# Second attention layer: added key blocks, quarter masks, and another order of VectorE's and GpSimd's work

## What is computed

```python
x = _layernorm(x + L0_attn(x))     # 16 heads of 8, queries and keys RMS-normed
x = _layernorm(x + L0_ffn(x))      # top-1 routing over 16 experts of 320 slots
x = _layernorm(x + L1_attn(x))     # causal attention, d_k 8, d_v 64
x = _layernorm(x + L1_ffn(x))      # three coupling cycles

def L1_attn(x):                    # x: [16, 256, 128], 16 heads
    scores = einsum('bhqd,bhkd->bhqk', q, k) / sqrt(8)
    scores = where(causal, -inf, scores)
    ctx = einsum('bhqk,bhkd->bhqd', softmax(scores), v)
    return ctx.transpose(0, 2, 1, 3).reshape(B, T, 16 * 64) @ Wo
```

## Time and profile before

| | us |
|---|---|
| median of 3 runs | 951.15 (950.95 to 953.62) |
| the profiled execution | 950.26 |
| its span | 948.5 |

### The profile page before, as it was taken

How to read it: one execution, slowest core, us unless ns; L and a number is a source line. 1 busy time by engine, 2 the same in 40 slices (tenths; PEclk the granted TensorE clock), 3 DMA queues, 4 the chain that set the end, 5 groups by cost and what they waited for, 6 DMA issues and landing times. The chain is left out here.

```text
span 948.5 us, 19520 instructions
## 1 busy us (share of the span) xinstructions
PE 790.8 (83%) x7061; PEld 451.7 (48%) x7061; DVE 575.1 (61%) x1715; ACT 472.5 (50%) x750; POOL 296.2 (31%) x437
## 2 busy tenths in 40 slices
PE   1588989998829999179999999999999999739970
PEld 0234444444316778125555555555555555534430
DVE  4458999999531111244576776666666656324687
ACT  0377888887812222035454545445455444306664
POOL 3012333333336000424344444434443322100152
PEclk9989999999958999679999999999999999878995
DMA  0274333433215553221454444333334332210002
GB/s 26 72 239 124 97 89 96 108 84 89 69 32 129 158 149 88 67 59 45 96 96 96 96 96 92 74 86 78 81 76 96 79 85 51 56 45 0 1 0 89
DMA packets 111705, 78.02 MB, mean 82 GB/s; under 512 B 12272, under 2 KB 103088, under 8 KB 111616
## 3 DMA queue, kind: packets, MB, share of 16 engines
q1 hardware_dynamic: 107984, 71.16, 30.5%
q0 software_dynamic: 3344, 5.56, 2.2%
q10 hardware_dynamic: 288, 0.13, 0.1%
HBM read 37.86 MB, written 13.63 MB: 54 GB/s over the span
## 5 line engine op out<-in xcount | busy, mean ns | idle before, releaser
L1375 DVE TENSOR_REDUCE l_neg_max<-l_by_query 128x6 bf16<-128x768 f32 x128 | 122.5, 957 | 129.9 <-PE l_by_query L1121 129.6
L1447 POOL TENSOR_SCALAR_AFFINE_SELECT l_probs<-l_probs 128x512 f32<-128x512 f32 x128 | 87.1, 680 | 190.9 <-ACT l_probs L1250 190.7
L493 ACT ACTIVATE l_probs<-l_ps_s,minus_bound 128x1024 f32<-128x1024 f32 x128 | 137.9, 1116 | 2.3 <-PE l_ps_s L367 1.4
L1250 ACT ACTIVATE l_probs<-l_by_key 128x768 f32<-128x768 f32 x128 | 103.8, 811 | 68.1 <-PE l_by_key L1151 63.9
L1166 PE MATMUL l_ps_c<-l_probs,l_values 128*64 128x256 f32 (+1 forms) x1024 | 113.5, 343 | 0.0
L1166 PEld LDWEIGHTS l_ps_c<-l_probs,l_values 128*64 128x64 f32 x1024 | 62.9, 138 | 39.7 <-issue 21.2
L1190 PE MATMUL l_ps_v<-w_o,l_ctx 128*128 128x128 f32 x512 | 68.6, 290 | 15.1 <-DVE l_ctx L1393 15.1
L382 PE MATMUL l_ps_o<-l_probs,l_vpad 128*32 128x256 f32 x1024 | 80.6, 397 | 0.2
L1103 PE MATMUL l_ps_v<-w_v,l_xT 128*128 128x512 f32 x128 | 72.8, 651 | 0.4 <-ACT l_values L1271 0.2
L1190 PEld LDWEIGHTS l_ps_v<-w_o,l_ctx 128*128 128x128 f32 x512 | 62.6, 200 | 20.9 <-DVE l_ctx L1393 15.5
L1271 ACT ACTIVATE l_values<-l_ps_v 128x512 f32<-128x512 f32 x64 | 38.2, 597 | 65.4 <-PE l_ps_v L1103 60.0
(11 more groups left out here) (229 smaller groups left out, 1422.5 us busy)
## 6 DMA issues: line engine op xcount, KB each, us to landing
l_rrep<-rden_d SPq DMA_DIRECT2D x32, 512.0 KB
q_ring<-l_parts SPq DMA_DIRECT2D x192, 64.0 KB
k_ring<-l_parts SPq DMA_DIRECT2D x192, 64.0 KB
w<-in_L_ffn_w_dram SPq DMA_DIRECT2D x32, 256.0 KB, 3.0
disp_d<-zeros SPq DMA_DIRECT2D x8, 320.0 KB, 3.7
l_xin<-in_L_attn_x_dram SPq DMA_DIRECT2D x16, 128.0 KB, 3.1
l_xr<-in_L_attn_x_dram SPq DMA_DIRECT2D x16, 128.0 KB, 2.5
x_d<-l_x SPq DMA_DIRECT2D x16, 128.0 KB, 2.1
```

The source lines that it names most:

```text
L493: act.activation(probs[c % RING][:, :], ps_s[c % 2][:, :], ACT.Exp, bias=k["minus_bound"][:, :], scale=SCALE).then_inc(probs_sb, 1)
L1250: act.activation(probs[c % P_RING][:, :, 0:N + P], by_key[:, :, 0:N + P], ACT.Exp, scale=SCALE).then_inc(p_sb, 1)
L1375: dve.tensor_reduce(neg_max[:, :, half, :, h].rearrange("p a u -> p u a"), by_query[:, :, 0:3 * P].rearrange("p u (a q) -> p u a q", a=3), ...
L1447: pool.affine_select(out=corners, in_=corners, compare_op=ALU.is_ge, fill=0.0, base=0, pattern=[[0, 4], [1, P]], channel_multiplier=-1).th ...
```

## The change

Four edits in the second layer:

1. `denominators` reads 256 columns of `probs` and no second block. For that GpSimd gets `add_blocks(b, c)`: after the context of pair c it adds key block 1 into the last 128 columns of block 0, in place. The denominators wait for the addition (`both_sb`); TensorE counts every context, not every second. The ring of `probs` grows from 4 to 6 and is counted through across batches.
2. The mask of `scores_by_query` is four matmuls on quarters of the array (64 rows by 64 columns), from a constant `corner`: two of 256 columns for queries 0 to 63, two of 128 columns for queries 64 to 127, of which only keys 64 to 127 need a mask.
3. TensorE's extra tasks are moved: the denominators one cycle later or more (0 from cycle 2 to 3, 1 from 4 to 5, 2 from 6 to 7, 3 from cycle 8 to cycle 1 of the next step), `x_by_channel` from the head of cycle 1 to behind the context, the first `maxima_by_head` from cycle 5 to 4, and the scores by query one pair further ahead.
4. VectorE, GpSimd and ScalarE follow in another order. VectorE's step now begins with `maxima(b + 1, 2)`.

```diff
-P_RING = 4
+P_RING = 6
@@ constants
-            pool.affine_select(out=k["causal"][:, :].rearrange("p (a b) -> p a b", b=P), ...
+            for half in range(2):
+                rows = k["corner"][64 * half:64 * half + 64, :].rearrange("p (a b) -> p a b", b=P)
+                pool.affine_select(out=rows, in_=rows, compare_op=ALU.is_ge, fill=-1e30,
+                                   base=0, pattern=[[0, 2], [-1, P]], channel_multiplier=1).then_inc(cut, 1)
@@ scores_by_query
                     for u in two:
-                        pe.matmul(by_query[:, u, P:3 * P], ident_bf[:, :], k["causal"][:, 0:2 * P],
+                        r = slice(64 * u, 64 * u + 64)
+                        pe.matmul(by_query[0:64, u, P:3 * P], ident_bf[r, r], k["corner"][r, :],
+                                  start=True, stop=False, skip_group_check=True)
+                    for u in two:
+                        r = slice(64 - 64 * u, 128 - 64 * u)
+                        later = by_query[64:128, u, P:3 * P].rearrange("p (a k) -> p a k", k=P)[:, :, 64:P]
+                        pe.matmul(later, ident_bf[r, r], k["corner"][r, :].rearrange("p (a k) -> p a k", k=P)[:, :, 0:64],
                                   start=True, stop=False, skip_group_check=True)
@@ denominators
-                    for kb, first, q0 in ((0, 0, 0), (1, N, P)):
-                        for g in range(4):
-                            u, e = divmod(g, 2)
-                            last = pe.matmul(ps_d[32 * g:32 * g + 32, q0:N], sums[:, j, :],
-                                             probs[(2 * j + e) % P_RING][:, u, first:first + N - q0],
-                                             start=j == 0 and kb == 0, stop=j == QUADS - 1 and kb == 1)
+                    pe.wait_ge(both_sb, b * PRE + 2 * j + 2)
+                    for g in range(4):
+                        u, e = divmod(g, 2)
+                        last = pe.matmul(ps_d[32 * g:32 * g + 32, 0:N], sums[:, j, :],
+                                         probs[(b * PRE + 2 * j + e) % P_RING][:, u, 0:N],
+                                         start=j == 0, stop=j == QUADS - 1)
@@ step of TensorE, as it is after
+                scores_by_key(b, 2);     context(b, 0); denominators(b - 1, 3); x_by_channel(b + 2); scores_by_query(b + 1, 2)
+                scores_by_key(b, 3);     context(b, 1); queries_keys(b + 2);                         scores_by_query(b + 1, 3)
+                scores_by_key(b, 4);     context(b, 2); denominators(b, 0);  values_of(b + 1, 0);    scores_by_query(b + 1, 4)
+                scores_by_key(b, 5);     context(b, 3); maxima_by_head(b + 1, 0); values_of(b + 1, 1); scores_by_query(b + 1, 5)
+                scores_by_key(b, 6);     context(b, 4); denominators(b, 1);  values_of(b + 1, 2);    scores_by_query(b + 1, 6)
+                scores_by_key(b, 7);     context(b, 5); values_of(b + 1, 3);                         scores_by_query(b + 1, 7)
+                scores_by_key(b + 1, 0); context(b, 6); denominators(b, 2);  project(b - 1, 0);      scores_by_query(b + 2, 0)
+                scores_by_key(b + 1, 1); context(b, 7); project(b - 1, 1);   maxima_by_head(b + 1, 1); scores_by_query(b + 2, 1)
@@ step of VectorE
+                maxima(b + 1, 2)
                 reciprocals(b - 1)
+
                 add_attention(b - 2)
-                maxima(b + 1, 1)
-
-                add_expert(b + 3)
-                maxima(b + 1, 2)
+                maxima(b + 1, 3)
+
+                lower_parts(b + 2)
+                maxima(b + 1, 4)
 
                 third_input(b - 2)
-                lower_parts(b + 2)
-                maxima(b + 1, 3)
-
-                second_input(b + 3)
-                maxima(b + 1, 4)
+                maxima(b + 1, 5)
 
                 divide(b - 1, 0)
                 divide(b - 1, 1)
-                maxima(b + 1, 5)
+                maxima(b + 1, 6)
 
                 divide(b - 1, 2)
                 divide(b - 1, 3)
-                maxima(b + 1, 6)
-
                 maxima(b + 1, 7)
+
+                add_expert(b + 3)
                 maxima(b + 2, 0)
+
+                second_input(b + 3)
+                maxima(b + 2, 1)
@@ GpSimd
+            def add_blocks(b, c):
+                if real(b):
+                    pool.wait_ge(ctx_ps, b * PRE + c + 1)
+                    pr = probs[(b * PRE + c) % P_RING]
+                    pool.tensor_tensor(pr[:, :, P:N], pr[:, :, P:N], pr[:, :, N:N + P], ALU.add).then_inc(both_sb, 1)
...
                 mask(b, 2)
+                add_blocks(b, 0)
+                mask(b, 3)
                 root(pow3, x3_step, (b - 2) * X3 + 1 + 2 * NB, mv3, veps3, rstd3, b - 2)
-                mask(b, 3)
-                root(pow2, x2_step, (b + 3) * X2 + 3 * NB, mv2, veps2, rstd2, b + 3)
+                add_blocks(b, 1)
                 mask(b, 4)
                 low_part(b + 2)
+                add_blocks(b, 2)
                 mask(b, 5)
+                add_blocks(b, 3)
+                mask(b, 6)
+                add_blocks(b, 4)
+                mask(b, 7)
                 gather(b + 4)
-                mask(b, 6)
-                mask(b, 7)
+                add_blocks(b, 5)
                 mask(b + 1, 0)
+                add_blocks(b, 6)
+                root(pow2, x2_step, (b + 3) * X2 + 3 * NB, mv2, veps2, rstd2, b + 3)
                 mask(b + 1, 1)
+                add_blocks(b, 7)
```

More of the change, by code:

```diff
@@ L157, in _ @@
                                base=0, pattern=[[1, P]], channel_multiplier=-1).then_inc(cut, 1)
[L159 to L162, removed]
+            pool.wait_ge(cut, 2)
+            for half in range(2):
+                rows = k["corner"][64 * half:64 * half + 64, :].rearrange("p (a b) -> p a b", b=P)
+                pool.affine_select(out=rows, in_=rows, compare_op=ALU.is_ge, fill=-1e30,
+                                   base=0, pattern=[[0, 2], [-1, P]], channel_multiplier=1).then_inc(cut, 1)
         @block.tensor
@@ L178, in _ @@
             s.did(dve.tensor_copy(k["gate_T"][:, :], gps[:, :]))
-            dve.wait_ge(cut, 3)
+            dve.wait_ge(cut, 4)
             s.did(dve.tensor_copy(k["ident_bf"][:, :], k["ident"][:, :]))
@@ L1168, in context @@
                                              pr[:, u, first:first + N - q0], start=kb == 0, stop=kb == 1)
-                    if c % 2:
-                        last.then_inc(ctx_ps, 1)
+                    last.then_inc(ctx_ps, 1)
             def denominators(b, j):
@@ L1195, in step @@
             def step(b):
-                x_by_channel(b + 2)
                 scores_by_key(b, 2)
                 context(b, 0)
-                scores_by_query(b + 1, 1)
+                denominators(b - 1, 3)
+                x_by_channel(b + 2)
+                scores_by_query(b + 1, 2)
                 scores_by_key(b, 3)
                 context(b, 1)
-                denominators(b, 0)
                 queries_keys(b + 2)
-                scores_by_query(b + 1, 2)
+                scores_by_query(b + 1, 3)
                 scores_by_key(b, 4)
                 context(b, 2)
+                denominators(b, 0)
                 values_of(b + 1, 0)
-                scores_by_query(b + 1, 3)
+                scores_by_query(b + 1, 4)
                 scores_by_key(b, 5)
                 context(b, 3)
-                denominators(b, 1)
+                maxima_by_head(b + 1, 0)
                 values_of(b + 1, 1)
-                scores_by_query(b + 1, 4)
+                scores_by_query(b + 1, 5)
                 scores_by_key(b, 6)
                 context(b, 4)
-                maxima_by_head(b + 1, 0)
+                denominators(b, 1)
                 values_of(b + 1, 2)
-                scores_by_query(b + 1, 5)
+                scores_by_query(b + 1, 6)
                 scores_by_key(b, 7)
                 context(b, 5)
-                denominators(b, 2)
                 values_of(b + 1, 3)
-                scores_by_query(b + 1, 6)
+                scores_by_query(b + 1, 7)
                 scores_by_key(b + 1, 0)
                 context(b, 6)
+                denominators(b, 2)
                 project(b - 1, 0)
-                scores_by_query(b + 1, 7)
+                scores_by_query(b + 2, 0)
                 scores_by_key(b + 1, 1)
                 context(b, 7)
-                denominators(b, 3)
                 project(b - 1, 1)
                 maxima_by_head(b + 1, 1)
-                scores_by_query(b + 2, 0)
+                scores_by_query(b + 2, 1)
             steps(step)
```

21 lines of the change are left out of this document (11 added, 10 removed).

## The result

The changed kernel takes 1019.99 us (median of 4 runs, 1017.28 to 1020.89) against 951.89 for the kernel before (4 runs, 950.95 to 953.62): a ratio of 1.0736, interval 1.0704 to 1.0769. The prediction was 982, with 997 as its upper end. The direction was right, the size was not: +68 us instead of +31.

What follows compares the result with a forecast made beforehand. The step was taken to be a loop through TensorE's cycles 7 and 8, the reciprocals and SyncE's queue. Growth of 26.9, plus 4.8 at the layer's end, less 0.5, gave +31.2 us: 982 us, range 955 to 997.

Steps and rivals of the forecast that it cites:

- The loop: Second layer's step: TensorE's cycles 7 and 8, one maxima, reciprocals, SyncE's queue, TensorE again; grows 2.07 to 27.7 us; chance 0.76.
- TensorE's own work: TensorE's busy time in one step of the kernel before, without its wait of 0.33: 25.16 us.
- GpSimd, the step that failed: Additions in GpSimd's order: denominators 0 wait 2.2 us in cycle 3 behind the root, costing nothing within the longer step.
- the sum: Whole time: +26.9 for thirteen steps, +4.8 at the layer's end, -0.5 for batches 0 and 14, so +31.2 us.
- The additions: Eight in-place additions a step on GpSimd, 0.65 us each, 5.2 us a step in all.
- Denominators: TensorE's denominator calls without the second key block: 0.58 instead of 0.79 us each, four calls, -0.84 a step.
- The mask: Quarter matmuls in the scores by query, side by side: -0.11 us a call, eight calls, -0.88 a step.
- TensorE's sum: TensorE's work per step after the change: 25.16 less 0.84 for denominators and 0.88 for the mask, 23.44 us.
- the rival at 924: TensorE bounds all through, so its smaller work gains 2.19 us a step: -27, 924 us; chance 0.09.
- The clock: Rival: TensorE's clock falls to half in the new waits, 35 us more over 13 steps, 1017 us; chance 0.05.
- The TensorE rival: TensorE's queue is the bound throughout, so less work there makes the kernel faster, 924 us; chance 0.09.
- The ends: Layer's end, with batch 14's later denominators: +4.8 us, bounds +2 and +6; steps of batches 0 and 14 together -0.5.

Runs made afterwards that it cites:

- g2: Changed kernel with gather last, root behind mask 4, early reciprocals, divisions behind maxima of head 6, denominators 3 in cycle 8, row maxima earlier on SyncE: 946.2 us.

## Why the prediction was right and wrong

- *The loop*: right. The 25.16 of TensorE's own work appeared as 25.15 once the row maxima went sooner; the stretch from the reciprocals through SyncE's queue was 16.74 where I took 16.6; the steps without the gather's wait were 27.2 to 28.0 against 27.7, with 11.16 from the scores of head 0 to the reciprocals against 11.14.
- *GpSimd, the step that failed*: I followed denominators 0 back to their addition, found the root ahead of it and got 2.2 (measured 2.20). I did not do the same for denominators 1 to 3. The gather, which the diff leaves between mask 7 and addition 5, costs its copy and two indirect DMAs, 713.22 to 716.51, ahead of that addition: a wait of 2.6 in cycle 7, inside the loop, which the sum had at nothing. It is there in ten steps, 24.8 us. With the half clock that fell into cycle 7 in three steps (batches 2, 6 and 12), 6.5 us, cycle 7 has 31.3 us that the prediction didn't have: 26.9 + 31.3 = 58.2, of 60.2 measured in the thirteen steps that it counts (batches 1 to 13; the last 2 are not taken apart). Moving the gather gave 33 back. "Occupancy covers it, order need not" was written and then applied once out of four times.
- *The additions*: 0.72 to 0.73 alone (I took 0.65), 1.15 to 1.16 in some, those beside divisions among them. GpSimd was busy 56% in the middle steps, near the 60 foretold.
- *Denominators*: a call takes 0.57 (717.29 to 717.86), I had 0.58.
- *The mask*: -0.88 was wrong; about zero for seven of eight calls. I had counted 0.16 for a new tile shape in the denominators, but not that the quarters bring one ahead of the mask. The mask itself is shorter by 0.08 to 0.10, near the 0.11 that I took. By the Trainium skill, "TensorEngine Tiling (Array Packing)", Gotcha 1, different row tiles can't access one PSUM bank at the same time, which would have left about half; the rows don't bear that out, and the two pairs of quarters start 0.01 apart. TensorE's sum was 24.04, not 23.44: 0.83 of the 0.88 is missing, and 0.22 came back in cycle 8, which is 3.65 where the prediction's own terms without the mask's gain give 3.87 (not taken apart). There was no loss from it in after, where TensorE wasn't the bound; the rival at 924 had 0.6 a step too much.
- *The clock*: the rival was given 0.05 because no wait would be as long as 3.68. Waits of 2.2 and 2.6 were enough: after has a stretch near 0.50 in nearly every step. Where it follows cycle 3, between the reciprocals and cycle 7, the queue covers it; only in three steps did it fall into cycle 7. The move of the root, which took the wait in cycle 3 away, brought it into the loop. That the rival's 1017 is so near to the measured 1020 is luck: it put 35 us of half clock into the loop, and the rows have 6.5.
- *The TensorE rival*: this kernel didn't reach its time, but a later one came near: with the loops cut, 23.92 a step and 932, its middle steps beginning 3.4 us later than in the kernel before (470.06 instead of 466.62).
- *The ends*: behind the step of batch 14, 3.4 instead of the 4.8 foretold. The step of batch 14 itself grew by 3.4 (25.14 to 28.56), where at most 0.5 was foretold. Up to batch 1 it is +0.1: the step of batch 0 won 2.4, but the layer's scores by key begin 2.5 later (424.19 instead of 421.70).

## What to carry to other kernels

For each wait that a change adds, follow the producer's own instruction list upward, once for every place where it is waited for; one checked case says nothing of the others, and a long instruction of another stage in that list is what costs. Then ask whether the wait lies inside or outside the loop that sets the step: here 2.6 us inside, with what followed from them, were 33 us of time, and 2.2 plus a slower clock outside gave little or nothing back when they were taken away. A wait outside can also hide something: taken away, it let the slower clock into the loop (986 became 1009). And before rebuilding a layer, try the one late transfer: two transfers sent two loads earlier in a queue were worth about as much as the work saved on TensorE.

## What was not expected of the hardware

- A quarter-array mask behind whole-array matmuls gained next to nothing: 0.08 saved in the mask, 0.09 lost before it, 0.05 won in a whole step of 25.1.
- After gaps of 2.6 us in cycle 7 and 2.2 in cycle 3, TensorE was granted 1.2 instead of 2.4 GHz for most of 3.4 us in after, and in the kernel with both moves in the whole of the windows from 714.0 to 719.1.
- VectorE's divisions and GpSimd slow each other: a division took 774 ns on average before and 887 after, four in a row 3.89 us in g2, a mask 1.00 instead of 0.64 and an addition 1.16 instead of 0.72 beside them. The Trainium skill, "SBUF — State Buffer", Who interferes with whom, says so of VectorE instructions with two SBUF inputs; these rows agree.
